# Another PSUM bank for two gate projections, one gate silu earlier on ScalarE, and the next activations loaded ahead of the weight stores

## Chip, cores and metric

The kernel runs on one core of a Trainium2 chip. The metric is the device time of one execution in microseconds; three executions of the kernel before took 3425.89 to 3429.51 us, with a median of 3427.64 us.

## What is computed

A layer over 128 sequences of 32 positions and 512 channels (4096 tokens): a conditional mixing of the 32 positions, a Mamba2-like attention part whose result is added to x, and a grouped convolution with a quantised 512x512 matrix behind it. The change lies in the attention part only:

```python
proj = jnp.einsum('bld,pd->blp', hidden_states, in_proj_w)      # gate | x, B, C | dt
xBC  = jax.nn.silu(causal_conv4(hbc))                           # 4 taps along the 32 positions
y    = scan(dt, A, x, B, C) + x * D                             # per head, 32 steps
yn   = y * rsqrt(mean(y*y over a group of 512) + eps) * norm_weight * jax.nn.silu(gate)
out  = jnp.einsum('bli,di->bld', yn, out_proj_w)
```

There are 8 groups of 512 inner channels (8 heads each); normalisation is over a group, so that the groups are independent until the output projection sums them.

## The kernel before

**Tiling.** The attention part runs 64 iterations: 8 groups (g), and in each 8 blocks of 512 tokens (j). In an iteration every engine has a program written out by hand (`attend` in `tensor_part`, `scalar_part` and `vector_part`, `scan_pass` in `gpsimd_part`, `step` in `sync_part`), and they meet through semaphores that count up over the whole kernel. Nothing is moved by a scheduler: each engine executes in the order written. `PE` is TensorE, `ACT` ScalarE, `DVE` VectorE, `POOL` GpSimd, `SP` the queue of SyncE that issues the DMAs.

**Precision.** A matrix is held as a high and a low part, and a product is three passes of matmuls (PASSES): one projection (`project(n)`, L1150 to L1157) is 12 matmuls of 512 columns into one PSUM bank, with the operands `ht` (the block's activations, turned, 2 MB, loaded by `load_h`, L984) and `wt`.

**The iteration on PE** (L1188 to L1252): projections 0 to 5 (B, C and four x tiles) into banks 0, 1, 2 in turn, with the sum of decay segments after the fourth; projections 6 and 7, the first two gates, into banks 0 and 1; the products of B and C into bank 3 (L1208); the x tiles turned into banks 4, 5, 6, 7 (`turn_x`, XT); projection 8, the third gate, into bank 2; the scan (L1172), 128 small products that write all of banks 0 to 3; the next group's raw weights turned into banks 5 and 6 (L1230, `prepare`, NEXT; not in the last group); projection 9, the fourth gate, into bank 4; and the output projection (L1249, "OUT"), for each of four channel tiles c twelve matmuls, three for each token tile t into bank OUT[t], which is (7, 5, 6, 4). Ahead of the last c the squares are turned into bank 3 (L1240). PROJ_BANK (L87) names each projection's bank.

**Waits on PE in this place.** The third gate needs bank 2 to have been read by the convolution (s_conv). The scan needs the scan matrix m (s_m), the turned x in SBUF (s_dtx), and the first three gates out of banks 0 to 2 (s_z, L1222). OUT needs for each c the low part of gy (s_ulo), and in c = 0 for bank 4 the fourth gate's silu (s_z, L1245), for banks 5 and 6 that DVE has read the turned weights (s_nlo, L1247). The next iteration's first projection needs `ht` (s_ht, L1188).

**The others.** ACT evicts a projection with its first tap (`tap`), takes silus (`silu`; `gate(c)`, L1276, from the gate's bank into z), copies the turned x to SBUF (L1320, dtx), multiplies by D (`skip`), copies the high parts (`high`, L1283; `next_high`, L1300) and squares y (`square`). DVE has the other taps, the scan matrix (L1421), y (`add_skip`, L1455), z times y (`gated`, L1463), the low parts (`low`, L1445; `next_low`, L1439), sums of squares (L1470) and, in the gaps, the decoding of an 8-bit weight table. SP issues all of the part's DMAs in order; a wait in it holds back whatever is issued later. `turn` is the last block of a group, in which the next group's weights are loaded, one by one as the projections are done.

Of the kernel before, what the change touches and what calls it, by code (L numbers as in the profile page):

```python
# [31 lines left out]
NBLK = TOK // BLK  # L32
TT = BLK // P
# [8 lines left out]
CT = GI // P  # L42
# [22 lines left out]
NCV = 2 + CT  # L65
# [18 lines left out]
CTX_AT = X2_AT + 4 * TT * DM  # L84
BIAS_AT = CTX_AT + 4 * TOK

PROJ_BANK = (0, 1, 2, 0, 1, 2, 0, 1, 2, 4)  # L87


class Shared:  # L90
# [765 lines left out]
def attend_part(nc, a, sh, ctx):  # L856
# [38 lines left out]
    sh.acc_at = TOP + WT_BYTES + HT_BYTES  # L895

    bank = sh.bank
    XT, SEG, CB, OUT, SSQ, NEXT = (4, 5, 6, 7), (4, 5), 3, (7, 5, 6, 4), 3, (5, 6)
    scanned = sh.low_banks


# [16 lines left out]
    s_proj = sem("s2_proj")  # L918
    s_tap = sem("s2_tap")
    s_cvstep = sem("s2_cvstep")  # L920
    s_conv = sem("s2_conv")
    s_silu = sem("s2_silu")
    s_z = sem("s2_z")
# [5 lines left out]
    s_dtx = sem("s2_dtx")  # L929
# [23 lines left out]
    NPJ = NCV + CT  # L953
# [26 lines left out]
    def sync_part(sp):  # L980
        acc_v = sh.acc_d.rearrange("(j t p) d -> j p t d", t=TT, p=P)

        def load_h(j):
            sp.dma_start(ht[:, :, :, :].rearrange("p a k n -> p (a k n)").bitcast(F32), sh.h_d[j]).then_inc(s_ht, 16)  # L984

        def next_chunks(j):

            return 2 + j, (j % 2 if j < NBLK - KC else NPJ + j - (NBLK - KC))

        def load_raw(g, j):  # L990
            for u, n in enumerate(next_chunks(j)):
                sp.dma_start(stage[u][:, :], weight_rows(a, n, g)).then_inc(s_raw[u], 16)

        x_v = a["x"].rearrange("b i d -> (b i) d").rearrange("(j t p) d -> j p t d", t=TT, p=P)

        def step(g, j, last, first=False):
            it = NBLK * g + j
            over = last and j == NBLK - 1
            nxt = g + 1
            turn = j == NBLK - 1 and not last  # L1000
            sp.wait_ge(s_accst, 16 * it + 16)
            if not last:
                load_raw(nxt, j)
            if turn:
                sp.wait_ge(s_nst, 32 * it + 32)
            if not first:
                sp.dma_start(acc[:, :, :], acc_v[j]).then_inc(s_accin, 16)
            if turn:
                for n in range(NPJ - 1):
                    sp.wait_ge(s_proj, NPJ * it + n + 1)  # L1010
                    sp.dma_start(wt[:, n, :, :, :].rearrange("p a k n -> p (a k n)").bitcast(F32),
                                 sh.wt_d[ds(g, 1), n].rearrange("o p n -> p (o n)")).then_inc(s_wt[n], 16)
                    if n == NCV:
                        sp.wait_ge(s_conv, NCV * (it + 1))
                        load_conv_params(nxt, sp)
            if over:
                sp.wait_ge(s_proj, NPJ * it + 7)
                sp.dma_start(sh.w4_nat[:, :, :].rearrange("p t i -> p (t i)"), sh.w4_d).then_inc(sh.s_w, 16)
                x2p_v = sh.acc_d.rearrange("(j b i) (s m) -> j s i b m", b=BLK // L, i=L, s=R)
                for h in range(2):  # L1020
                    bs = slice(h * BLK // L // 2, (h + 1) * BLK // L // 2)
                    for s in range(R):
                        sp.dma_start(sh.x2p0[s * L:(s + 1) * L, bs, 1:1 + P], x2p_v[0, s, :, bs, :]).then_inc(sh.s_x2p[0][h], 16)
                sp.dma_start(sh.x2_0[:, :, :, :].rearrange("p t r m -> p t (r m)"), acc_v[0]).then_inc(sh.s_x2[0], 16)
            if not last:
                sp.wait_ge(s_nlo, 2 * it + 2)
                for u, n in enumerate(next_chunks(j)):
                    sp.dma_start(sh.wt_d[ds(g, 1), n].rearrange("o p n -> p (o n)"),
                                 wnext[:, u, :, :].rearrange("p a n -> p (a n)").bitcast(F32)).then_inc(s_nst, 16)
            sp.wait_ge(s_proj, NPJ * (it + 1))  # L1030
            if not over:
                load_h((j + 1) % NBLK)
            if first:
                for t in range(TT):
                    sp.wait_ge(s_ulo, CT * it + t + 1)
                    sp.dma_start(z[:, t, :], x_v[j, :, t, :]).then_inc(s_xin[t], 16)
            if over:
                sp.dma_start(sh.ctx_all[:, :], sh.ctxb_d.rearrange("b o -> (b o)").partition_broadcast(P)).then_inc(sh.s_par, 16)
                sp.dma_start(sh.bias[:, :], a["L0_ffn_bias"].partition_broadcast(P)).then_inc(sh.s_par, 16)
            if turn:  # L1040
                n = NPJ - 1
                sp.wait_ge(s_nst, 32 * it + 64)
                sp.dma_start(wt[:, n, :, :, :].rearrange("p a k n -> p (a k n)").bitcast(F32),
                             sh.wt_d[ds(g, 1), n].rearrange("o p n -> p (o n)")).then_inc(s_wt[n], 16)
                sp.wait_ge(s_u, CT * (it + 1))
                load_d_norm(nxt, sp)
                sp.wait_ge(s_out, TT * (it + 1))
                for k in range(KC):
                    sp.dma_start(wot[:, :, :, k * P:(k + 1) * P].rearrange("p a c n -> p (a c) n").bitcast(F32),
                                 sh.wt_d[ds(g, 1), NPJ + k].rearrange("o p (a n) -> p (o a) n", n=P)).then_inc(s_wot, 16)  # L1050
            sp.wait_ge(s_acc, TT * it + 2 * TT)
            sp.dma_start(acc_v[j], acc[:, :, :]).then_inc(s_accst, 16)

        sp.sem_inc(s_nst, 32)
        sp.wait_ge(sh.s_turned, NWC)
        for j in range(NBLK):
            step(0, j, False, first=True)
        with sp.Fori(1, G - 1) as g:
            for j in range(NBLK):
                step(g, j, False)  # L1060
        for j in range(NBLK):
            step(G - 1, j, True)
        sp.wait_ge(s_nst, 32 * NBLK * (G - 1) + 32)
# [82 lines left out]
    def tensor_part(pe):  # L1146
        def attend(g, j, prepare):
            it = NBLK * g + j

            def project(n):  # L1150
                pe.wait_ge(s_wt[n], 16 * g + 16)
                pb = bank[PROJ_BANK[n]]
                for q, (l, rr) in enumerate(PASSES):
# [60 lines left out]
            for t in range(TT):  # L1214
                turn_x(t)

            pe.wait_ge(s_conv, NCV * it + NCV)
            project(NCV + CT - 2)

            pe.wait_ge(s_m, SEGB * it + 2 * SEGB)  # L1220
            pe.wait_ge(s_dtx, TT * it + TT)
            pe.wait_ge(s_z, CT * it + CT + 3)  # L1222
            for c in range(CT):
                ins = scan(c)
            ins.then_inc(s_yp, 1)
# [9 lines left out]
            for c in range(CT):  # L1235
                if c == CT - 1:
                    pe.wait_ge(s_y, CT * it + 2 * CT)
                    pe.wait_ge(s_sqsum, (CT - 1) * (it + 1))
                    for t in range(TT):
                        ins = pe.transpose(bank[SSQ][:, t * P:(t + 1) * P], y[:, 0, t * P:(t + 1) * P], sh.ident[:, :])  # L1240
                    ins.then_inc(s_sqturn, 1)
                pe.wait_ge(s_ulo, CT * it + c + 1)
                for t in range(TT):
                    if c == 0 and OUT[t] == PROJ_BANK[NCV + CT - 1]:
                        pe.wait_ge(s_z, CT * it + 2 * CT)  # L1245
                    elif c == 0 and prepare and OUT[t] in NEXT:
                        pe.wait_ge(s_nlo, 2 * it + NEXT.index(OUT[t]) + 1)  # L1247
                    for q, (l, rr) in enumerate(PASSES):
                        ins = pe.matmul(bank[OUT[t]][:, :], gy[:, c, l, t * P:(t + 1) * P], wot[:, rr, c, :],  # L1249
                                        start=(c == 0 and q == 0), stop=(c == CT - 1 and q == 2))  # L1250
                    if c == CT - 1:
                        ins.then_inc(s_out, 1)  # L1252
# [13 lines left out]
    def scalar_part(act):  # L1266
        def attend(g, j, prepare, first=False):
            it = NBLK * g + j
# [5 lines left out]
            def gate(c):  # L1274
                act.wait_ge(s_proj, NPJ * it + NCV + c + 1)
                act.activation(z[:, c, :], bank[PROJ_BANK[NCV + c]][:, :], ACT.Silu).then_inc(s_z, 1)  # L1276

# [3 lines left out]
            def high(c):  # L1281
                act.wait_ge(s_u, CT * it + c + 1)
                act.activation(gy[:, c, 0, :], z[:, c, :], ACT.Copy).then_inc(s_uhi, 1)  # L1283

            def square(c):
                act.activation(y[:, c, :], y[:, c, :], ACT.Square).then_inc(s_sq, 1)


            def tap(n):
                act.wait_ge(s_proj, NPJ * it + n + 1)  # L1290
                if n == 0:
                    act.wait_ge(s_cvp, 16 * NCP * g + 16 * NCP)
                act.activation(xc[:, n, :], bank[PROJ_BANK[n]][:, :], ACT.Identity, bias=cvb[:, n:n + 1],  # L1293
                               scale=cvw[:, n, TAPS - 1:TAPS]).then_inc(s_tap, 1)
# [33 lines left out]
            high(0)  # L1328
            next_high(1)
            square(0)  # L1330
            high(1)
            square(1)
            gate(3)
            high(2)
            square(2)
            high(3)
# [626 lines left out]
```

## Time and profile before

| | |
|---|---|
| runs | 3425.89, 3427.64, 3429.51 us |
| profiled execution: time, span | 3422.22 us, 3420.4 us |
| mean granted clock of TensorE | 0.997 |
| PE busy | 3325.6 us (97%) |
| DVE busy | 2610.5 us (76%) |
| ACT busy | 1762.6 us (52%) |
| POOL busy | 737.1 us (22%) |
| DMA engines, mean rate | 136 GB/s |

The span is from the first to the last instruction, and 1.8 us lie around it. A matmul's busy time contains its latency and overlaps the next one's start, so a group of matmuls "ends" in the timeline a little after the next group begins; PEld is the weight load, which runs ahead of its matmul. A line "idle before <- releaser" names what an engine waited for. The attention part is from 110 us to 3143 us, in 64 iterations.

### The profile page before, as it was taken

The page shows a single profiled execution, that of the slowest core. Times are in us where ns is not written, and L with a number is a line of the kernel's source. Part 1 is how long each engine was busy: PE and PEld are TensorE (multiplying, and loading weights), DVE is VectorE, ACT ScalarE, POOL GpSimd, SP SyncE. Part 2 cuts the span into 40 slices and gives each one's busy share as a digit, 9 for nine tenths or more (in the row PEclk, how much of TensorE's full clock was granted, in tenths as well). Part 3 has the DMA queues.
Part 4 walks back from the last instruction along what each step waited for, and adds up shares of the span by engine and source line. Part 5 has one row for each costly group of instructions (what it writes and reads, how often), then busy time and mean ns, then how long its engine had stood idle before and what let it go on. Part 6 is the DMA issues. An engine that isn't in the chain of part 4 may idle for free. (4 is left out here: it accounts for less than half of the span.)

```text
span 3420.4 us, 86449 instructions
## 1 busy us (share of the span) xinstructions
PE 3325.6 (97%) x33306; PEld 2726.9 (80%) x33306; DVE 2610.5 (76%) x4367; ACT 1762.6 (52%) x3203; POOL 737.1 (22%) x520
## 2 busy tenths in 40 slices
PE   8999999999999999999999999999999999999999
PEld 6777777778778878777788788787787877888888
DVE  6787778878787887878888777888878878787443
ACT  5666665555555555555555555555555555554111
POOL 1122221122211222112221122211122212221333
PEclk9999999999999999999999999999999999999999
DMA  7432363325533263334433253334433352224331
GB/s 268 167 116 92 135 215 130 122 104 182 174 117 123 99 220 135 123 116 159 160 135 130 109 200 119 135 133 169 145 111 135 137 171 98 74 98 154 93 92 59
DMA packets 207793, 466.29 MB, mean 136 GB/s; under 512 B 35134, under 2 KB 80606, under 8 KB 198284
## 3 DMA queue, kind: packets, MB, share of 16 engines
q1 hardware_dynamic: 206364, 464.72, 38.9%
q0 software_dynamic: 368, 0.85, 0.1%
q10 hardware_dynamic: 1024, 0.27, 0.0%
q8 instruction: 18, 0.29, 0.0%
q14 instruction: 19, 0.16, 0.0%
HBM read 313.68 MB, written 152.09 MB: 136 GB/s over the span
## 5 line engine op out<-in xcount | busy, mean ns | idle before, releaser
L1155 PE MATMUL low_banks<-ht,wt 128*128 128x512 f32 x6912 | 1616.5, 391 | 18.9 <-DMA ht<-h_d 13.6
L1155 PEld LDWEIGHTS low_banks<-ht,wt 128*128 128x128 f32 x6912 | 1289.0, 188 | 305.1 <-issue 28.2
L1403 DVE SCALAR_TENSOR_TENSOR xc<-low_banks,cvw,xc 128x496 f32<-128x496 f32 (+2 forms) x1152 | 824.1, 717 | 238.6 <-ACT xc L1293 210.5
L1249 PE MATMUL bank<-wot,gy 128*128 128x512 f32 x3072 | 749.9, 396 | 6.7
L1249 PEld LDWEIGHTS bank<-wot,gy 128*128 128x128 f32 x3072 | 562.3, 188 | 159.8 <-ACT z L1276 32.6
L1293 ACT ACTIVATE xc<-low_banks,cvb,cvw 128x512 f32<-128x512 f32 x384 | 298.5, 779 | 517.9 <-PE low_banks L1155 517.9
L1092 POOL TENSOR_TENSOR r<-rv,neg_half 128x4 f32<-128x4 f32 x64 | 98.2, 1534 | 1841.6 <-DVE rv L1493 1841.6
L1073 POOL TENSOR_TENSOR segr<-adts,mask_le 128x1024 fp32r<-128x1024 f32 x128 | 242.8, 1917 | 349.7 <-DVE adts L1394 349.7
L1272 ACT ACTIVATE xc<-xc 128x512 f32<-128x512 f32 x384 | 240.6, 626 | 140.2 <-DVE xc L1403 139.5
L1455 DVE TENSOR_TENSOR y<-xc,low_banks 128x512 f32<-128x512 f32 x256 | 174.0, 680 | 159.7 <-issue 159.7
L1283 ACT ACTIVATE gy<-z 128x512 fp32r<-128x512 f32 x256 | 161.9, 633 | 245.7 <-DVE z L1463 245.7
L1172 PEld LDWEIGHTS low_banks<-m,dtx 32*64 32x64 f32 x16384 | 169.2, 130 | 75.1 <-ACT z L1276 71.0
L1087 POOL TENSOR_TENSOR y<-y,step_of 128x512 f32<-128x512 f32 x128 | 162.8, 1291 | 299.5 <-ACT y L1309 299.5
L1172 PE MATMUL low_banks<-m,dtx 32*64 32x32 f32 x16384 | 176.5, 226 | 47.8 <-ACT z L1276 44.0
L1505 DVE SCALAR_TENSOR_TENSOR acc<-bank,r,acc 128x512 f32<-128x512 f32 x256 | 176.7, 745 | 26.2 <-ACT acc L1347 15.3
L1463 DVE SCALAR_TENSOR_TENSOR z<-z,nw,y 128x512 f32<-128x512 f32 x256 | 190.6, 745 | 6.7
L1155 PE MATMUL bank<-ht,wt 128*128 128x512 f32 x768 | 195.6, 404 | 0.0
L1445 DVE TENSOR_TENSOR gy<-z,gy 128x512 fp32r<-128x512 f32 x256 | 175.9, 687 | 13.5
L1753 PE MATMUL p_y<-wq,x3t 128*128 128x512 f32 x768 | 182.9, 394 | 0.0
L1276 ACT ACTIVATE z<-low_banks 128x512 f32<-128x512 f32 x192 | 113.5, 591 | 127.1 <-PE low_banks L1155 127.1
L1279 ACT ACTIVATE xc<-xc,dsk 128x512 f32<-128x512 f32 x256 | 171.5, 727 | 0.0
L1753 PEld LDWEIGHTS p_y<-wq,x3t 128*128 128x128 f32 x768 | 141.9, 188 | 28.3
(195 smaller groups left out, 3469.6 us busy)
## 6 DMA issues: line engine op xcount, KB each, us to landing
ht<-h_d SPq DMA_DIRECT2D x63, 2048.0 KB, 9.2
acc_d<-acc SPq DMA_DIRECT2D x64, 1024.0 KB, 4.3
wt_d<-wnext SPq DMA_DIRECT2D x112, 512.0 KB, 3.4
acc<-acc_d SPq DMA_DIRECT2D x56, 1024.0 KB, 7.0
wt<-wt_d SPq DMA_DIRECT2D x70, 512.0 KB, 7.1
stage<-in_L_attn_in_proj_w SPq DMA_DIRECT2D x84, 256.0 KB, 2.7
wot<-wt_d SPq DMA_DIRECT2D x28, 512.0 KB, 8.4
xb<-in_x SPq DMA_DIRECT2D x8, 1024.0 KB, 7.3
```

Source lines behind the costliest of these rows:

```text
L1073: pool.tensor_tensor(segr[:, half, :, :], adts[:, half, :].bitcast(F32).unsqueeze(2).to_broadcast([P, TT * HG, L]), sh.mask_le[:, :].unsqu ...
L1155: ins = pe.matmul(pb[:, :], wt[:, n, l, k, :], ht[:, rr, k, :], start=(q == 0 and k == 0), stop=(q == 2 and k == KC - 1))
L1172: ins = pe.matmul(scanned[u * HP:(u + 1) * HP, b, (c * TT + t) * L:(c * TT + t + 1) * L], dtx[rows, t, h * HP:(h + 1) * HP], m[rows, t, h, ...
L1249: ins = pe.matmul(bank[OUT[t]][:, :], gy[:, c, l, t * P:(t + 1) * P], wot[:, rr, c, :], start=(c == 0 and q == 0), stop=(c == CT - 1 and q ...
L1272: act.activation(xc[:, n, :], xc[:, n, :], ACT.Silu).then_inc(s_silu, 1)
L1293: act.activation(xc[:, n, :], bank[PROJ_BANK[n]][:, :], ACT.Identity, bias=cvb[:, n:n + 1], scale=cvw[:, n, TAPS - 1:TAPS]).then_inc(s_tap, 1)
L1403: ins = dve.scalar_tensor_tensor(dst, src, cvw[:, n, TAPS - 1 - k:TAPS - k], dst, ALU.mult, ALU.add)
L1445: dve.tensor_tensor(gy[:, c, 1, :], z[:, c, :], gy[:, c, 0, :].bitcast(F32), ALU.subtract).then_inc(s_ulo, 1)
L1455: dve.tensor_tensor(by_residue(y[:, c, :]), by_residue(xc[:, 2 + c, :]), scanned[:, :, c * P:(c + 1) * P].rearrange("p b (t l) -> p b t l" ...
L1463: dve.scalar_tensor_tensor(z[:, c, :], z[:, c, :], nw[:, c:c + 1], y[:, c, :], ALU.mult, ALU.mult).then_inc(s_u, 1)
L1505: dve.scalar_tensor_tensor(acc[:, t, :], bank[OUT[t]][:, :], r[:, t:t + 1], acc[:, t, :], ALU.mult, ALU.add).then_inc(s_acc, 1)
L1753: ins = pe.matmul(p_y[t % 2][q][:, :], x3t[:, l, t, r, :], wq[:, q, rr, r, :], start=(n == 0 and r == 0), stop=(n == 2 and r == R - 1))
```

## The change

PROJ_BANK puts the third gate into bank 4 (where the first turned x tile lay) instead of bank 2, and the fourth gate into bank 7 instead of bank 4. PE's wait ahead of the third gate is for the first turned x tile to be in SBUF (s_dtx), and the wait for the last convolution moves down to the scan, which now waits for two gates instead of three. The output banks are used in the order 4, 5, 6, 7, and in c = 0 the first of them waits for the third gate's silu, the last for the fourth's. On ACT, `gate(3)` stands behind `square(0)` instead of behind `square(1)`. On SP, `load_h` of the next block stands ahead of the wait for, and the stores of, the next group's weights.

```diff
-PROJ_BANK = (0, 1, 2, 0, 1, 2, 0, 1, 2, 4)
+PROJ_BANK = (0, 1, 2, 0, 1, 2, 0, 1, 4, 7)
...
-    XT, SEG, CB, OUT, SSQ, NEXT = (4, 5, 6, 7), (4, 5), 3, (7, 5, 6, 4), 3, (5, 6)
+    XT, SEG, CB, OUT, SSQ, NEXT = (4, 5, 6, 7), (4, 5), 3, (4, 5, 6, 7), 3, (5, 6)
...
+            sp.wait_ge(s_proj, NPJ * (it + 1))
+            if not over:
+                load_h((j + 1) % NBLK)
             if not last:
                 sp.wait_ge(s_nlo, 2 * it + 2)
                 for u, n in enumerate(next_chunks(j)):
                     sp.dma_start(sh.wt_d[ds(g, 1), n].rearrange("o p n -> p (o n)"),
                                  wnext[:, u, :, :].rearrange("p a n -> p (a n)").bitcast(F32)).then_inc(s_nst, 16)
-            sp.wait_ge(s_proj, NPJ * (it + 1))
-            if not over:
-                load_h((j + 1) % NBLK)
...
-            pe.wait_ge(s_conv, NCV * it + NCV)
+            pe.wait_ge(s_dtx, TT * it + 1)
             project(NCV + CT - 2)
 
             pe.wait_ge(s_m, SEGB * it + 2 * SEGB)
             pe.wait_ge(s_dtx, TT * it + TT)
-            pe.wait_ge(s_z, CT * it + CT + 3)
+            pe.wait_ge(s_z, CT * it + CT + 2)
+            pe.wait_ge(s_conv, NCV * it + NCV)
...
-                    if c == 0 and OUT[t] == PROJ_BANK[NCV + CT - 1]:
-                        pe.wait_ge(s_z, CT * it + 2 * CT)
+                    if c == 0 and OUT[t] in PROJ_BANK[NCV + CT - 2:]:
+                        pe.wait_ge(s_z, CT * it + CT + 3 + PROJ_BANK[NCV + CT - 2:].index(OUT[t]))
...
             square(0)
+            gate(3)
             high(1)
             square(1)
-            gate(3)
             high(2)
```

How it moves the instructions, first on PE between the turned x tiles and the first output matmuls of an iteration of the first seven groups. The names: xc the convolved tiles, ht and wt a projection's operands, m and dtx the scan's, stage the next group's raw weights, wot and gy the output projection's; low_banks are banks 0 to 3. Before:

```order
L1162 MATMUL bank7<-ident,xc_52 128x128 x4
L1155 MATMUL low_banks<-ht_58,wt_57 128x512 [waits s2_wt8,s2_conv]
L1155 MATMUL low_banks<-ht_58,wt_57 128x512 x11
L1222 REGISTER_ALU [waits s2_dtx,s2_scan_matrix]
L1172 MATMUL low_banks<-m_86,dtx_85 64x32 [waits s2_z]
L1172 MATMUL low_banks<-m_86,dtx_85 64x32 x127
...
L1155 MATMUL bank4<-ht_58,wt_57 128x512 [waits s2_wt9]
L1155 MATMUL bank4<-ht_58,wt_57 128x512 x11
L1242 REGISTER_ALU
L1249 MATMUL bank7<-wot_69,gy_82 128x512 [waits s2_ulo]
```

After:

```order
L1162 MATMUL bank7<-ident,xc_52 128x128 x4
L1217 REGISTER_ALU
L1155 MATMUL bank4<-ht_58,wt_57 128x512 [waits s2_wt8,s2_dtx]
L1155 MATMUL bank4<-ht_58,wt_57 128x512 x11
L1222 REGISTER_ALU [waits s2_dtx,s2_scan_matrix]
L1172 MATMUL low_banks<-m_86,dtx_85 64x32 [waits s2_conv,s2_z]
L1172 MATMUL low_banks<-m_86,dtx_85 64x32 x127
...
L1155 MATMUL bank7<-ht_58,wt_57 128x512 [waits s2_wt9]
L1155 MATMUL bank7<-ht_58,wt_57 128x512 x11
L1246 REGISTER_ALU [waits s2_ulo]
L1250 MATMUL bank4<-wot_69,gy_82 128x512 [waits s2_z]
```

The order of the work is the same; the bank of both gates, what each waits for, and the bank that is filled first are other.

On ACT, behind the copies of the turned weights in the same iteration (y the squares, gy the high parts). Before:

```order
L1286 ACTIVATE y_54<-y_54 128x512
L1283 ACTIVATE gy_82<-z_53 128x512 [waits s2_u]
L1286 ACTIVATE y_54<-y_54 128x512
L1275 REGISTER_ALU
L1276 ACTIVATE z_53<-bank4 128x512 [waits s2_proj]
L1283 ACTIVATE gy_82<-z_53 128x512 [waits s2_u]
```

After:

```order
L1287 ACTIVATE y_54<-y_54 128x512
L1276 REGISTER_ALU
L1277 ACTIVATE z_53<-bank7 128x512 [waits s2_proj]
L1284 ACTIVATE gy_82<-z_53 128x512 [waits s2_u]
L1287 ACTIVATE y_54<-y_54 128x512
L1284 ACTIVATE gy_82<-z_53 128x512 [waits s2_u]
```

The fourth gate's silu has moved up by one high part and one square.

On SP, around the load of the next block's activations in the first group. Before:

```order
L1028 DMA wt_d<-wnext_70 128x1024 [waits s2_nlo]
L1028 DMA wt_d<-wnext_70 128x1024
L984 DMA ht_58<-h_d 128x4096 [waits s2_proj]
L1036 DMA z_53<-in_x 128x512 [waits s2_ulo] x4
L1052 DMA acc_d<-acc_59 128x4x512 [waits s2_acc]
```

After:

```order
L984 DMA ht_58<-h_d 128x4096 [waits s2_proj]
L1031 DMA wt_d<-wnext_70 128x1024 [waits s2_nlo]
L1031 DMA wt_d<-wnext_70 128x1024
L1036 DMA z_53<-in_x 128x512 [waits s2_ulo] x4
L1052 DMA acc_d<-acc_59 128x4x512 [waits s2_acc]
```

The 2 MB load stands ahead of the two 0.5 MB stores and their wait.

## Rows read from the trace of the kernel before

**Rows 1.** The page, busy time: engine, us, share of the span, instructions
```profile
PE 3325.6 (97%) x33306; PEld 2726.9 (80%) x33306; DVE 2610.5 (76%) x4367; ACT 1762.6 (52%) x3203; POOL 737.1 (22%) x520
```

**Rows 2.** Who waited for whom, whole kernel: us in total, times, longest us
```profile
PEld bank L1249 <- ACT z L1276: 32.6, 62, 0.5
...
PE low_banks L1172 <- ACT z L1276: 44.0, 64, 0.7
...
PEld bank L1249 <- DVE wnext L1439: 11.1, 55, 0.2
PE low_banks L1155 <- DMA ht<-h_d: 13.6, 22, 1.1
...
PE low_banks L1172 <- issue: 3.8, 2, 2.0
```

**Rows 3.** Timeline of PE, one iteration's second half: start, duration, group, idle before
```profile
1658.15 3.00 PE L1155 MATMUL low_banks<-ht,wt 128*128 128x512 f32 x12
1661.83 2.74 PE L1172 MATMUL low_banks<-m,dtx 32*64 32x32 f32 x256 [0.69 <-ACT z L1276]
...
1665.35 3.02 PE L1155 MATMUL bank<-ht,wt 128*128 128x512 f32 x12
1668.21 8.82 PE L1249 MATMUL bank<-wot,gy 128*128 128x512 f32 x36
1676.87 0.60 PE L1240 MATMUL low_banks<-ident,y 128*128 128x128 f32 x4
1677.22 2.99 PE L1249 MATMUL bank<-wot,gy 128*128 128x512 f32 x12
1680.59 11.19 PE L1155 MATMUL low_banks<-ht,wt 128*128 128x512 f32 x48 [0.37 <-DMA ht<-h_d]
```

**Rows 4.** Timeline of ACT in the same iteration
```profile
1657.12 2.07 ACT L1320 ACTIVATE dtx<-bank 128x512 f32<-128x512 f32 x4 [0.38 <-PE bank L1162]
...
1661.18 0.60 ACT L1276 ACTIVATE z<-low_banks 128x512 f32<-128x512 f32 x1 [0.78 <-PE low_banks L1155]
...
1667.26 0.62 ACT L1286 ACTIVATE y<-y 128x512 f32<-128x512 f32 x1
1668.90 0.63 ACT L1283 ACTIVATE gy<-z 128x512 fp32r<-128x512 f32 x1 [1.01 <-DVE z L1463]
...
1669.95 0.58 ACT L1276 ACTIVATE z<-bank 128x512 f32<-128x512 f32 x1
```

**Rows 5.** Timeline of DVE in the same iteration
```profile
1656.66 1.29 DVE L1421 TENSOR_TENSOR m<-low_banks,y 128x512 f32<-128x512 f32 x2 [0.70 <-PE low_banks L1208]
...
1668.78 0.68 DVE L1439 TENSOR_TENSOR wnext<-bank,wnext 128x512 fp32r<-128x512 f32 x1
...
1669.98 0.68 DVE L1445 TENSOR_TENSOR gy<-z,gy 128x512 fp32r<-128x512 f32 x1
...
1675.10 0.69 DVE L1470 TENSOR_TENSOR y<-y 128x512 f32<-128x512 f32 x1
```

**Rows 6.** Timeline of SP in the same iteration
```profile
1669.64 0.91 SPq L1028 DMA_DIRECT2D wt_d<-wnext  x2
1670.69 0.62 SPq L984 DMA_DIRECT2D ht<-h_d  x1
```

**Rows 7.** Timeline of PE in the very first iteration
```profile
150.28 8.37 PE L1249 MATMUL bank<-wot,gy 128*128 128x512 f32 x36
158.49 0.60 PE L1240 MATMUL low_banks<-ident,y 128*128 128x128 f32 x4
```

**Rows 8.** Tile ht: loads' landing times, 1660 to 2770 us, then the last group
```profile
DMA to landing us min/median/max: 8.9/9.4/10.5
...
DMA to landing us min/median/max: 7.7/7.9/8.7
```

**Rows 9.** The core: span and mean granted clock
```profile
core 0: 3420.4 us, clock 0.997
```

**Rows 10.** One stretch: us, busy (x instructions) of PE, PEld, DVE, ACT, POOL, PEclk, DMA, GB/s
```profile
2804.00:2807.00 3.00, 3.00 (x8) 2.32 (x8) 2.80 (x5) 2.10 (x4) 0.00 (x0) 0.50 0.01 3
```

## The prediction

> **What bounds the kernel now.** I read the page first: TensorE is busy for 97% of the span [rows 1]. So the kernel is bound by TensorE's stream, and a change can give at most what that stream loses in gaps. The second view is therefore the list of waits, sorted by who waits [rows 2]: PE itself waits 44.0 us in 64 pieces ahead of the scan for ScalarE's silu of the third gate, and 13.6 us in 22 pieces for the activations `ht`. The weight loads of the output projection wait another 32.6 us in 62 pieces for a silu (the fourth gate's) and 11.1 us in 55 for VectorE's reading of the turned weights. All four waits lie in the second half of an iteration. The third view is the timeline of each engine there [rows 3 to 6]; the reader is to see on it who is how late, because everything that is released by the scan moves along with it.
>
> A gap costs a little more than its row says. Where nothing waits, a group's modelled end overruns the next group's start: 1665.35 + 3.02 = 1668.37, while the next begins at 1668.21 [rows 3], so 0.16 us of overlap are lost as well each time that PE waits.
>
> **Third gate in bank 4.** Before, the scan may start only when the third gate has left bank 2, since it writes banks 0 to 3. The projection ends at 1661.15, the silu runs from 1661.18 to 1661.78, the scan starts at 1661.83 [rows 3, 4]. With the gate in bank 4 the silu runs beside the scan. What the scan waits for otherwise is long done: m at 1657.95 [rows 5], the four turned tiles at 1659.19 [rows 4]; the convolution and the first two gates are ahead of these on their engines. So the next limit is PE itself, and each iteration gains 0.69 + 0.16 = 0.85 us: 64 x 0.85 = **54.4 us**. The bounds: 44.0, the rows' own time, and 55.
>
> The new wait of the third gate is for the first of the four copies that start at 1657.12 and take 2.07 together [rows 4]; a single one of this shape ends about 0.6 later, at 1657.7. PE gets there at 1658.15 [rows 3]: a margin of 0.4 us, cost nothing. Behind this wait stand all of PE's later work; if the margin vanished, each 0.1 us would cost 6.4 us. The fourth gate goes into bank 7, whose turned tile left by 1659.19: no cost. One more register instruction on PE ahead of the third gate: none of the like ahead of other projections leaves a gap, cost nothing.
>
> **Output banks and the fourth gate's silu.** Before, the last bank of c = 0 waits for a silu that runs from 1669.95 to 1670.53, behind `high(1)` and `square(1)` [rows 4]. How much do this and the wait for the turned weights cost PE, which both show only at the weight loads? The 36 matmuls take 1676.87 - 1668.21 = 8.66 us here [rows 3]. In the very first iteration, where PE had been held up and the others were ahead, they take 158.49 - 150.28 = 8.21 us [rows 7]. So both waits cost 0.45 us. By the time of the weight loads' waits, 32.6 to 11.1 [rows 2], 0.34 of it is the silu's; I take 0.38, since the other is only 0.2 at a time and partly hidden by the matmul that runs. Now the silu follows `square(0)`, which ends at 1667.88, and PE's projection, which ends at 1668.37: it runs from about 1668.4 to 1669.0, while bank 7 is wanted at 1668.21 + 9 x 0.228 = 1670.3 (0.228 being 8.21 / 36). The wait goes. Gain: 62 x 0.38 = **23.6 us**, bounds 62 x 0.34 = 21 and 62 x 0.45 = 28. The first bank's new wait is for the third silu, done seven us earlier: nothing.
>
> What is late next? The wait for the turned weights stays: VectorE ends at 1669.46 [rows 5], both it and PE hang on the scan. Then c = 1, wanted at 1668.21 + 12 x 0.228 = 1670.95, with its weight load 0.2 earlier; its low part ends at 1670.66 [rows 5]. A margin of 0.1 to 0.3; if it is missed by 0.2 in 56 iterations, 11 us come back. The sums of squares end at 1675.79 [rows 5] and PE wants them at 1676.87 - 0.38 = 1676.49: enough. `high(1)` on ScalarE started at 1668.90 for want of VectorE; now it stands behind the silu, free at about 1668.95: nothing.
>
> **The load ahead of the stores.** SP issued the stores at 1669.64 and the load at 1670.69, though the projections had ended at 1668.37 [rows 3, 6]: the load is issued 2.2 us earlier. PE's second half is shorter by 0.4 after that point, so the load is wanted at 1677.22 + 2.83 - 0.38 = 1679.67 and has some 11.2 us. It lands in 8.9 to 10.5 us with stores ahead of it, in 7.7 to 8.7 in the last group, which has none [rows 8]. Even the slowest is in time. The 22 waits go: 13.6 + 22 x 0.16 = **17.1 us**; bounds 13.6, and 18. The stores land later, behind 2 MB; who waits for them (the next iteration's `next_high`, and at a group's end the load of the fourth gate's weights, used some 40 us later) has time. At a group's end SP could issue the output weights a little late; they are wanted at the products of B and C, 22 us into the next iteration.
>
> **Sum.** 54.4 + 23.6 + 17.1 = 95.1 us. The profiled execution took 3422.2 us and would take 3327; the median of the runs stands 5.4 us above it, so I forecast 3427.6 - 95.1 = 3332 as the median. Not in the sum: in the first group PE also waits for VectorE's convolution, which hangs on loads of x behind the same queue. These may come up to 1 us earlier, or PE's shorter half may be given back there; eight iterations, -3 to +4 us.
>
> **The rivals.**
> - *The clock comes back too* (0.06). At the scan's first execution in two places PE waits 3.8 us for "issue", beside the 0.69 for the silu [rows 2], and after it TensorE's granted clock is 0.50, the 1.2 GHz level: 8 matmuls in 3 us [rows 10]. All stretches at that level in the span are worth 3420.4 x 0.003 = 10 us [rows 9]. If the shorter idle time no longer brings them about, up to half of that, 5 us, is gained too: 3327. The Trainium skill (TensorE: Matmul & The Clock Gate, What's actually happening) says that an idle array falls to the lower clock and activity releases it. By that rule fewer waits can only help, and the time would be 3327 or so instead of 3332. The rows speak against more: 64 waits of 0.69 did not bring the mean below 0.997.
> - *One term doesn't come* (0.14). The low part of c = 1, or VectorE's weights, holds up the output projection as long as the silu did (3356), or the load still lands late because loads and stores share the engines in another way (3349), or the scan finds another wait of some tenths (3345). For it: margins of 0.1 to 0.4. Against it: each margin is larger than the spread that I see between iterations.
> - *The third gate isn't freed* (0.03). If something else lets the scan start at the old time, only 41 us are left: 3387. Nothing in the rows supports it.
> - *ScalarE stuck behind the fourth gate: slower* (0.02). ScalarE executes in order, so `gate(3)` now holds `high(1)` until PE has done the fourth projection. If that came late, the low part, the output projection and everything behind would shift. The row has `high(1)` at 1668.90 and DVE taking up the low part at 1669.98; 0.4 us are hidden, 0.2 more lie ahead of PE's c = 1. To lose the 95 us, 1.5 us per iteration, and 7 more, the silu would have to end 2.2 us later than 1669.0. From there on the kernel is slower; at 3 us of delay it would be 3427.6 - 95 + 64 x 2.4 = 3486. The projection ends at 1668.37, so I see no way to it.
>
> **How the numbers follow.** The forecast itself has 0.75. Its bounds alone give 3427.6 - 101 - 4 = 3323 to 3427.6 - 79 = 3349. The range takes in the clock at the lower end with 3 us for the spread of the medians, and the single failing terms at the upper: 3318 to 3354. Below 0.2% (7 us) a measurement of this kernel can't tell a change from none. Faster by more than that 0.96, within it 0.02, slower 0.02.
>
> **What would show it.** The wait of L1172 for the silu vanishes from PE's list, and from the third gate's start to the scan's start it is 2.84 us instead of 3.68. The 36 output matmuls take 8.2 to 8.3 us, without a wait for a silu. `ht` is issued right at the end of the fourth gate's projection, and PE's waits for it are gone. PE's busy share rises to about 99%, and an iteration is 1.2 us shorter, besides the waits for ht. Wrong would be: a wait of the third gate's projection for dtx, of L1250 for gy, or an iteration shorter by under 0.8 us.

## The result, and the profile after

| | before | changed |
|---|---|---|
| median of 4 runs each | 3426.86 us | 3331.30 us |
| lowest to highest | 3425.89 to 3429.51 | 3330.59 to 3335.74 |
| profiled execution: time, span | 3422.22, 3420.4 us | 3330.75, 3329.0 us |
| PE busy | 3325.6 us (97%) | 3293.0 us (99%) |
| mean granted clock of TensorE | 0.997 | 0.997 |

The ratio is 0.9723 with a 95% interval of 0.9706 to 0.974: 95.6 us less by the medians, 91.5 us in the profiled executions. In a second comparison, beside the last experiment, the same kernel gave 0.9739 (0.9725 to 0.9753). The time lies in the forecast range, 0.7 us from the forecast.

Who waited for whom on PE (total us, times, longest us) in the changed kernel, the counterpart of [rows 2]:

```profile
PE low_banks L1155 <- DVE xc L1404: 9.3, 9, 1.9
...
PE low_banks L1172 <- issue: 4.0, 2, 2.2
...
PE bank L1250 <- DVE gy L1446: 1.2, 7, 0.2
```

The waits for the third gate's silu (44.0 us) and for ht (13.6 us) are not there any more, and the output projection waits for no silu. The first line has grown: in the kernel before PE waited for the convolution (xc) 4.8 us in 8 pieces.

The timeline of PE in the same iteration as in [rows 3], from its start:

```profile
1588.54 11.09 PE L1155 MATMUL low_banks<-ht,wt 128*128 128x512 f32 x48
...
1611.79 1.97 PE L1162 MATMUL bank<-ident,xc 128*128 128x128 f32 x16
1613.51 3.00 PE L1155 MATMUL bank<-ht,wt 128*128 128x512 f32 x12
1616.44 2.74 PE L1172 MATMUL low_banks<-m,dtx 32*64 32x32 f32 x256
...
1619.95 3.02 PE L1155 MATMUL bank<-ht,wt 128*128 128x512 f32 x12
1622.82 8.40 PE L1250 MATMUL bank<-wot,gy 128*128 128x512 f32 x36
1631.05 0.60 PE L1241 MATMUL low_banks<-ident,y 128*128 128x128 f32 x4
1631.41 3.00 PE L1250 MATMUL bank<-wot,gy 128*128 128x512 f32 x12
1634.24 2.48 PE L1155 MATMUL low_banks<-ht,wt 128*128 128x512 f32 x10
```

From the third gate's start to the scan's it is 2.93 us (3.68 before), the 36 output matmuls take 8.23 us (8.66 before), and the next iteration starts 2.83 us after the last group of twelve (3.37 before, in an iteration that waits for ht). The silu of the third gate runs beside the scan, that of the fourth ahead of the second high part, on ACT, as against [rows 4]:

```profile
1616.55 0.60 ACT L1277 ACTIVATE z<-bank 128x512 f32<-128x512 f32 x1 [0.78 <-PE bank L1155]
...
1621.87 0.62 ACT L1287 ACTIVATE y<-y 128x512 f32<-128x512 f32 x1
1623.02 0.60 ACT L1277 ACTIVATE z<-bank 128x512 f32<-128x512 f32 x1 [0.52 <-PE bank L1155]
1623.51 0.62 ACT L1284 ACTIVATE gy<-z 128x512 fp32r<-128x512 f32 x1
```

And SP issues the load 0.2 us after the output projection's start, where it was 2.5 us [rows 3, 6]:

```profile
1623.01 0.33 SPq L984 DMA_DIRECT2D ht<-h_d  x1
1624.26 0.91 SPq L1031 DMA_DIRECT2D wt_d<-wnext  x2
```

The iterations of groups 2 to 7 take 45.7 us each (47.3 before). The first group's eight take 382.1 us together (386.6 before), more than eight times 45.7, and this is where time was lost. The end of its seventh and the start of its eighth iteration on PE:

```profile
441.57 8.37 PE L1155 MATMUL low_banks<-ht,wt 128*128 128x512 f32 x36
451.89 4.61 PE L1155 MATMUL low_banks<-ht,wt 128*128 128x512 f32 x12 [1.95 <-DVE xc L1404]
```

PE waits 1.95 us for the convolution, and then twelve matmuls take 4.61 us instead of 3.00. The reason for the second stands in the granted clock of two stretches ahead of and behind the wait (columns as in [rows 10]):

```profile
445.00:449.00 4.00, 4.00 (x19) 3.31 (x18) 3.15 (x8) 3.97 (x6) 0.00 (x0) 1.00 0.00 0
452.50:455.50 3.00, 3.00 (x8) 2.30 (x7) 2.88 (x5) 1.30 (x3) 2.18 (x2) 0.50 0.59 178
```

It was at 2.4 GHz ahead of the wait and at 1.2 GHz after it.

### The profile page after: what moved, and what is told of

Same layout as the page of the kernel before. It is cut to its first block and busy times, and to the rows that moved or that the text cites. A ratio compares the mean times of both kernels' runs of the same rounds, so it can differ in the third digit from the quotient of the medians.

```text
span 3329.0 us, 86577 instructions
## 1 busy us (share of the span) xinstructions
PE 3293.0 (99%) x33306; PEld 2735.0 (82%) x33306; DVE 2609.7 (78%) x4367; ACT 1765.0 (53%) x3203; POOL 738.1 (22%) x520
## 5 line engine op out<-in xcount | busy, mean ns | idle before, releaser
L1155 PE MATMUL low_banks<-ht,wt 128*128 128x512 f32 x6144 | 1423.4, 390 | 9.3 <-DVE xc L1404 9.3
L1155 PEld LDWEIGHTS low_banks<-ht,wt 128*128 128x128 f32 x6144 | 1153.6, 188 | 258.6 <-DVE xc L1404 13.1
L1250 PE MATMUL bank<-wot,gy 128*128 128x512 f32 x3072 | 729.7, 393 | 1.2 <-DVE gy L1446 1.2
L1155 PE MATMUL bank<-ht,wt 128*128 128x512 f32 x1536 | 387.3, 401 | 0.0
L1155 PEld LDWEIGHTS bank<-ht,wt 128*128 128x128 f32 x1536 | 280.2, 189 | 55.8
L1446 DVE TENSOR_TENSOR gy<-z,gy 128x512 fp32r<-128x512 f32 x256 | 176.0, 687 | 15.2 <-ACT gy L1284 1.8
```

What stands on the lines that cost most here:

```text
L1155: ins = pe.matmul(pb[:, :], wt[:, n, l, k, :], ht[:, rr, k, :], start=(q == 0 and k == 0), stop=(q == 2 and k == KC - 1))
L1446: dve.tensor_tensor(gy[:, c, 1, :], z[:, c, :], gy[:, c, 0, :].bitcast(F32), ALU.subtract).then_inc(s_ulo, 1)
```

## The experiments

Ten runs follow, one of them of the change itself once more. All ratios are to the kernel before, which ran beside them with medians of 3421.66 to 3422.22 us (3426.86 beside the change's first run). Their intervals are 0.0013 to 0.0017 to each side (5 to 6 us), 0.001 for the silu alone, and 0.0024 (8 us) for the gate alone, whose four executions lie between 3362.73 and 3378.68 us. "Difference" is to the median of before. Where sums over an iteration's stretches are given below, they are start-to-start times of PE's timeline in the profiled executions, added up over all 64 iterations.

| third gate in bank 4 | earlier silu | load first | kernel | ratio | difference |
|---|---|---|---|---|---|
| yes | yes | yes | the change | 0.9723 and 0.9739 | -95.6 and -89.3 us |
| yes | yes | no | stores first | 0.9844 | -53.1 us |
| yes | no | yes | silu late | 0.9800 | -69.4 us |
| no | yes | yes | gate in bank 2 | 0.9882 | -40.1 us |
| yes | no | no | gate alone | 0.9850 | -50.2 us |
| no | yes | no | silu alone | 0.9986 | -4.2 us |
| no | no | yes | load alone | 0.9935 | -21.3 us |

### The stores first again

```diff
-            sp.wait_ge(s_proj, NPJ * (it + 1))
-            if not over:
-                load_h((j + 1) % NBLK)
             if not last:
                 sp.wait_ge(s_nlo, 2 * it + 2)
                 ...
+            sp.wait_ge(s_proj, NPJ * (it + 1))
+            if not over:
+                load_h((j + 1) % NBLK)
```

> The changed kernel with the weights' stores ahead of the load of ht again, as before. Theory (the load was late because it was issued 2.2 us later, behind 1 MB of stores): PE waits for ht at the start of an iteration again, and more than before, since the other two parts leave PE's second half 0.43 us shorter behind the load's issue: 29 of 48 iterations lost 0.6 us before, now some 32 us in all over groups 1 to 6; the first group gains back a few us. Time 3352 to 3362 us. Rival (with the shorter iteration the load is hidden anyway, DMA having more idle time at the end): no wait of PE for ht, 3331 us.

Measured: 3368.54 us, ratio 0.9844 (0.9828 to 0.9861). PE's list of waits:

```profile
PE low_banks L1155 <- DMA ht<-h_d: 30.4, 39, 1.8
PE low_banks L1155 <- DVE xc L1404: 5.3, 8, 0.8
```

The waits for ht are more than twice those of the kernel before. With the 0.16 us of lost overlap each, they are 30.4 + 39 x 0.16 = 36.6 us; with an early load they are nothing. The rival is out. The loss was still underestimated: 36 to 42 us by the ratios, where 21 to 31 had been expected. The traces show where it lies: the stretches from the last twelve output matmuls to the next iteration's start are 39.1 us longer than in the change, the first 48 projection matmuls of groups 2 to 8 another 3.7, and the first group's give back only 4.8.

### The silu late again

```diff
             square(0)
-            gate(3)
             high(1)
             square(1)
+            gate(3)
```

> The changed kernel with the fourth gate's silu behind high(1) and square(1) again. Theory (the silu's place on ScalarE is what held up the output bank): the 36 output matmuls take 8.6 us instead of 8.23, PEld waits 0.5 us for the silu in 62 iterations, and the time is 3331 + 62 x 0.38 = 3355 us. Rival (the bank order did it, the fourth bank now being the last in both): 3331 us.

Measured: 3352.25 us, ratio 0.98 (0.9784 to 0.9816). The weight loads' list, and PE's timeline of one iteration:

```profile
PEld bank L1250 <- ACT z L1277: 32.4, 63, 0.5
```

```profile
1680.11 8.83 PE L1250 MATMUL bank<-wot,gy 128*128 128x512 f32 x36
1688.77 0.60 PE L1241 MATMUL low_banks<-ident,y 128*128 128x128 f32 x4
```

The wait is back with 32.4 us, and 36 matmuls take 8.66 us. So it is the silu's place that held up the bank, and the order of banks is not enough: the fourth bank comes last in either order.

### The third gate in bank 2 again

```diff
-PROJ_BANK = (0, 1, 2, 0, 1, 2, 0, 1, 4, 7)
+PROJ_BANK = (0, 1, 2, 0, 1, 2, 0, 1, 2, 7)
...
-            pe.wait_ge(s_dtx, TT * it + 1)
+            pe.wait_ge(s_conv, NCV * it + NCV)
...
-            pe.wait_ge(s_z, CT * it + CT + 2)
-            pe.wait_ge(s_conv, NCV * it + NCV)
+            pe.wait_ge(s_z, CT * it + CT + 3)
```

> The changed kernel with the third gate in bank 2 again, and its old waits; the fourth stays in bank 7, the other two parts stay. Theory (the scan's wait for the third silu is a term by itself): PE waits 0.69 us in 64 iterations at L1172, third gate to scan 3.69 us instead of 2.93, and the time is 3331 + 64 x 0.76 = 3380 us. Rival (the parts overlap, so that part of it is hidden by slack behind the scan): under 3365 us.

Measured: 3381.59 us, ratio 0.9882 (0.9865 to 0.9898), so 49 to 54 us behind the change. The wait is back to the tenth:

```profile
PE low_banks L1172 <- ACT z L1276: 44.0, 64, 0.7
PE low_banks L1155 <- DVE xc L1403: 11.5, 9, 1.9
```

From the third gate's start to the scan's it is 3.68 us again, 48.5 us more over the 64 iterations. The term comes whole; nothing behind the scan had hidden a part of it.

### The gates' banks exchanged

```diff
-PROJ_BANK = (0, 1, 2, 0, 1, 2, 0, 1, 4, 7)
+PROJ_BANK = (0, 1, 2, 0, 1, 2, 0, 1, 7, 4)
...
-OUT = (4, 5, 6, 7)
+OUT = (7, 5, 6, 4)
...
-            pe.wait_ge(s_dtx, TT * it + 1)
+            pe.wait_ge(s_dtx, TT * it + TT)
```

> The changed kernel with the two gates' banks exchanged: the third gate in bank 7, the last turned tile's, so that it waits for all four copies to SBUF, the fourth in bank 4, output banks 7, 5, 6, 4. Theory (the first tile's bank is free 0.4 us ahead of need, the last one's 1.05 us behind it): PE waits 0.9 to 1.1 us ahead of the third gate in each iteration, time 3331 + 64 x 1.1 = 3401 us, so that the bank alone decides between a gain of 2.8% and one of under 1%. Rival (PE's queue waits there anyway, any of the four banks would do): 3331 us. The granted clock holds at 1.00 in spite of the wait in both.

Measured: 3404.29 us, ratio 0.9953 (0.9936 to 0.997). PE's timeline, and its list:

```profile
1740.45 1.97 PE L1162 MATMUL bank<-ident,xc 128*128 128x128 f32 x16
1743.26 3.04 PE L1155 MATMUL bank<-ht,wt 128*128 128x512 f32 x12 [0.84 <-ACT dtx L1321]
1746.23 2.74 PE L1172 MATMUL low_banks<-m,dtx 32*64 32x32 f32 x256
```

```profile
PE bank L1155 <- ACT dtx L1321: 54.0, 64, 0.8
```

From the turned tiles' start to the gate's it takes 2.81 us instead of 1.72: 1.09 us more in each of 64 iterations, 70 us. The choice among the four banks is worth 73 to 79 us: in the last tile's bank the gate waits longer than the scan did before. The mean granted clock stayed at 0.997 with this wait of 0.84 us in every iteration. The same run has a longer wait in its first group, and behind it the clock did not fall:

```profile
169.69 3.01 PE L1155 MATMUL low_banks<-ht,wt 128*128 128x512 f32 x12 [1.98 <-DVE xc L1404]
```

```profile
170.00:173.00 3.00, 3.00 (x15) 2.44 (x13) 2.89 (x5) 1.86 (x4) 2.86 (x3) 1.00 0.51 164
```

### Each part alone

The edits are those of the change, taken singly into the kernel before; for the first two the fourth gate is in bank 7 and the output banks are 4 to 7.

> The kernel before with only the third gate in bank 4 (fourth in bank 7, output banks 4 to 7; silu late, stores first). Theory: what PE gains ahead of the scan moves the issue of the load along with it, since the fourth projection and VectorE's reading of the turned weights both follow the scan; so the waits for ht stay at 14 us and the term comes whole, 49 us faster than before, ratio 0.9857. Rival (any time that PE gains is partly taken by the load): 25 to 35 us faster.

Measured: 3371.48 us, ratio 0.985 (0.9827 to 0.9874). PE waits for ht 11.8 us in 20 pieces, about as before. What PE gains ahead of the scan moves the load's issue along, and the rival (25 to 35 us) lies outside the interval of 42 to 59 us.

> The kernel before with only the output banks' order and the earlier silu (fourth gate in bank 7). Theory, after the run with the stores first lost 41 us instead of 17 (everything that shortens PE's work between the issue of the load and its use is taken back by the wait for ht where the load is late): the 36 output matmuls take 8.23 instead of 8.66 us, 26 us in all, but PE's waits for ht grow from 14 to about 30 us and more, so that only 3 to 8 us are left: ratio to before 0.998 to 0.999. Rival (terms add up): 25 us faster, ratio 0.993.

Measured: 3417.51 us, ratio 0.9986 (0.9976 to 0.9996). PE's list:

```profile
PE low_banks L1172 <- ACT z L1276: 44.0, 64, 0.7
PE low_banks L1155 <- DMA ht<-h_d: 28.8, 34, 1.8
```

The waits for ht have grown from 13.6 us in 22 pieces [rows 2] to 28.8 in 34, with the lost overlap by 15.2 + 12 x 0.16 = 17.1 us. That is not the whole: start to start, the stretches with this wait are 18.7 us longer, and the first 48 projection matmuls 3.0 us, half of it in the first group. Of the 25.4 us that the output matmuls gain, 4.2 reach the end (0.9986, 1 to 8 us by the interval).

> The kernel before with only the load of ht ahead of the stores. Theory: PE's 14 us of waits for ht go (18 us in start-to-start times), the first group gives back 3 to 6 us because its loads of x now land later behind the stores: 12 to 16 us faster, ratio 0.9955 to 0.9965. Rival (the load is worth the 41 us that its removal from the changed kernel cost): ratio 0.988.

Measured: 3400.36 us, ratio 0.9935 (0.9919 to 0.9952), 21.3 us instead of the 12 to 16 expected. No wait for ht is left, and the first group gives back only a little (PE waits 7.1 us for DVE's xc, 4.8 before). The traces tell where the rest is. The stretches with the wait are 18.6 us shorter, as expected (18). But where ht was late, the first 48 projection matmuls behind it were slower too: they took 11.00 to 11.02 us start to start (the 11.19 of [rows 3], the next group starting at 1691.61), where they take 10.93 with ht in time (the 11.09 of the changed kernel's timeline). In groups 2 to 8 that is 2.8 us more, the output matmuls add 1.3, and the first group gives back 2.3 instead of 3 to 6.

### The loads of x ahead of the stores

In the first group there is no residual in HBM yet, and SP loads x instead (four loads of 0.25 MB into z); they stood behind ht and the stores. ScalarE sorts them into acc, VectorE adds to it, and only then convolves the next projection. The edit moves them between the two:

```diff
             if not over:
                 load_h((j + 1) % NBLK)
+            if first:
+                for t in range(TT):
+                    sp.wait_ge(s_ulo, CT * it + t + 1)
+                    sp.dma_start(z[:, t, :], x_v[j, :, t, :]).then_inc(s_xin[t], 16)
             if not last:
                 sp.wait_ge(s_nlo, 2 * it + 2)
                 ...
-            if first:
-                for t in range(TT):
-                    sp.wait_ge(s_ulo, CT * it + t + 1)
-                    sp.dma_start(z[:, t, :], x_v[j, :, t, :]).then_inc(s_xin[t], 16)
```

> The changed kernel, in which the first group also issues its four loads of x ahead of the weights' stores. Theory (the first group's projections wait for VectorE's convolution, which hangs on ScalarE's sorting of x, which waits 1.5 to 3 us for loads that lie behind 1 MB of stores): ScalarE's wait for x goes from 17.7 to under 4 us, the first four projections of the first group take 11.0 to 11.5 us instead of 12.1 to 14.8, and the time falls by 8 to 12 us below the changed kernel's (ratio to before 0.969 to 0.970). Rival (the sorting's own 4.2 us are what is late): under 3 us.

Measured: 3319.42 us, ratio 0.9698 (0.9681 to 0.9714). How x landed in the changed kernel, in the tile's view from 150 to 500 us:

```profile
  DMA z<-in_x: 17.7, 8
...
DMA to landing us min/median/max: 6.9/9.5/10.8
```

and here, in the same view, where ScalarE's wait for x is gone:

```profile
DMA to landing us min/median/max: 3.9/6.5/9.0
```

In the second iteration of the changed kernel ScalarE waits 2.15 us before it sorts:

```profile
254.42 4.17 ACT L1348 ACTIVATE acc<-z 128x512 f32<-128x512 f32 x4 [2.15 <-DMA z<-in_x]
```

Here it begins to sort without a gap, and PE starts the next iteration and runs through:

```profile
251.38 4.17 ACT L1348 ACTIVATE acc<-z 128x512 f32<-128x512 f32 x4
```

```profile
249.98 2.99 PE L1250 MATMUL bank<-wot,gy 128*128 128x512 f32 x12
252.81 9.50 PE L1155 MATMUL low_banks<-ht,wt 128*128 128x512 f32 x41
```

Of PE's waits for DVE's xc one of 0.8 us is left. The first 48 projection matmuls of the first group's iterations take 88.6 us in all (100.5 in the change, 103.1 in its second run, 94.8 in the kernel before), 11.1 each, as expected. It is the loads that were late, not the sorting. This is the fastest of the kernels whose difference to the change is explained.

### The scan's waits moved into the projection

```diff
-            def project(n):
+            def scan_waits():
+                pe.wait_ge(s_m, SEGB * it + 2 * SEGB)
+                pe.wait_ge(s_dtx, TT * it + TT)
+                pe.wait_ge(s_z, CT * it + CT + 2)
+                pe.wait_ge(s_conv, NCV * it + NCV)
+
+            def project(n, before_last=None):
...
                 for q, (l, rr) in enumerate(PASSES):
+                    if q == 2 and before_last:
+                        before_last()
...
-            project(NCV + CT - 2)
-
-            pe.wait_ge(s_m, SEGB * it + 2 * SEGB)
-            pe.wait_ge(s_dtx, TT * it + TT)
-            pe.wait_ge(s_z, CT * it + CT + 2)
-            pe.wait_ge(s_conv, NCV * it + NCV)
+            project(NCV + CT - 2, scan_waits)
```

It is made on top of the kernel with x ahead of the stores. The change itself ran beside it.

> The changed kernel itself, on the chip of the other runs of this call, so that they can be compared with it: ratio to before 0.972 to 0.973. PE's start of the third gate to the start of the scan is 2.93 us, of which 0.1 stand as an issue wait of the first small weight load (0.35 us).

> The changed kernel with x loaded ahead of the stores in the first group, and with the scan's waits standing inside the third gate's projection, ahead of its last four matmuls, where all of them are met (the last copy to SBUF ends 1.0 us into the projection, these matmuls start at 1.8). Theory A (the 0.1 us ahead of the scan is the register arithmetic and the waits in PE's queue): third gate to scan takes 2.84 us instead of 2.93, the issue wait of the first small weight load goes, and the time is 6 us below the kernel with x ahead of the stores, ratio to before 0.968. Theory B (it is the change from the full array to tiles of 32 rows, whose first weights aren't loaded while a full-array matmul runs; the same 0.35 us stands ahead of the products of B and C in every iteration): 2.93 us stay, ratio 0.9698.

Measured: the change 3332.93 us, ratio 0.9739 (0.9725 to 0.9753); this kernel 3317.79 us, ratio 0.9695 (0.9682 to 0.9709). That is the same ratio as with x ahead of the stores alone, within the interval. PE's timeline and the weight loads':

```profile
1603.45 3.00 PE L1163 MATMUL bank<-ht,wt 128*128 128x512 f32 x12
1606.38 2.74 PE L1180 MATMUL low_banks<-m,dtx 32*64 32x32 f32 x256
```

```profile
1601.34 0.35 PEld L1216 LDWEIGHTS low_banks<-xc 128*32 128x32 f32 x32 [0.35 <-issue]
...
1606.38 2.63 PEld L1180 LDWEIGHTS low_banks<-m,dtx 32*64 32x64 f32 x256 [0.35 <-issue]
```

2.93 us stay, and so does the 0.35 us ahead of the first small weight load: theory A is out. Theory B is not shown. "Tiles of 32 rows" fits only one of its two places: the rows give 32x64 for the scan's weights, but 128x32 for those of the products of B and C, which have 128 rows and 32 columns. What both have in common is the step from 128x128 weights to smaller ones, and nothing here varied their size.

The Trainium skill (TensorE: Matmul & The Clock Gate, The mechanism) says that PE pulls a weight load ahead of running matmuls when it addresses other rows of the array or goes to the background weight buffer. The trace agrees for the full-array stream, which uses the same rows throughout: in the changed kernel the next iteration's weight loads start 0.22 us ahead of their first matmul (1634.24), while the twelve output matmuls still run (1631.41 + 3.00):

```profile
1634.02 2.50 PEld L1155 LDWEIGHTS low_banks<-ht,wt 128*128 128x128 f32 x11
```

Why the first small load is not pulled ahead in this way stays open.

## Why the prediction was right, and where it was not

The sum was 95.1 us; measured are 91.5 in the profiled executions, 95.6 and 89.3 by the medians. The mechanism was right: all three waits went, and each part taken back or taken alone moved the time as its wait says. That the median came within 0.7 us of the forecast is luck, since the parts erred on both sides. Start to start on PE, the traces of before and after give:

| stretch of an iteration | forecast, with its bounds | gained by the traces |
|---|---|---|
| third gate to scan | 54.4 (44 to 55) | 48.5 us |
| 36 output matmuls | 23.6 (21 to 28) | 26.1 us |
| last twelve output matmuls to the next iteration | 17.1 (13.6 to 18) | 18.6 us |
| first 48 projection matmuls, groups 2 to 8 | not in the sum | 2.5 us |
| the same, first group | not in the sum (3 gained to 4 lost) | 5.7 us lost |

- **The third gate in bank 4.** The part alone gave 50.2 us by the medians. The wait of 0.69 went whole. What was mis-sized is "the next limit is PE itself, and each iteration gains 0.69 + 0.16": of the lost overlap 0.06 came back instead of 0.16, since 0.1 is lost ahead of the scan's first small weight load, in every arrangement in which the scan didn't wait for the silu. The new wait cost nothing, as forecast, and its margin was there: the first copy ran from 1612.48 to 1613.08 and the gate started at 1613.51, 0.43 us later. In bank 7 the same gate costs 70 us.
- **Output banks and silu.** The change without the earlier silu was 20 to 26 us behind. The remaining wait for the turned weights costs less than was split off for it: 8.23 us are left against 8.21 in [rows 7], 0.02 instead of 0.07.
- **The load ahead of the stores.** All the waits went; alone it was 21.3 us. "Even the slowest is in time" held: the load has 11.2 us, and landed in 7.8 to 9.9. But 18.6 + 2.5 = 21.1 us lie outside the forecast's own bounds (13.6 to 18): PE's rows for ht leave out the shorter delays, and the projection behind a late ht was slower as well.
- **Left out of the sum: the first group.** This step failed. Its loads of x were expected up to 1 us earlier, and at worst 4 us were to be given back. They landed later, 9.5 us after their issue instead of 8.6 in the median and 10.8 instead of 9.9 at most, while PE's second half was shorter. PE's wait for the convolution went from 4.8 to 9.3 us, and 1.6 us were lost at the lower clock behind one wait of 1.95 us: 5.7 us in all, and 8.3 in the second run of the change. With x ahead of the stores the time is 8 to 14 us below the change's; that is more than the change had lost, since it also takes the waits for xc that the kernel before had.
- **The rivals.** None of them came: no term was missing, ScalarE was not stuck behind the fourth gate (the high part behind it starts at 1623.51, 0.69 after the output projection's start, exactly as before: 1668.90 - 1668.21). The clock's rival failed: both first executions of the scan still wait 4.0 us for "issue", and the mean clock is 0.997. The range was also narrower than its reason: "the single failing terms at the upper" end include 3356 us, and it stopped at 3354.

The parts aren't independent, which the sum did not say, though it used it. Alone they give 50.2 + 4.2 + 21.3 = 75.7 us, together 89 to 96. The missing 14 to 20 lie between silu and load: with the stores first, what PE gains behind the load's issue is turned into waiting for it. Gate and silu without the load give 53.1, about 50.2 + 4.2; gate and load give 69.4, about 50.2 + 21.3; silu and load give 40.1, far more than 4.2 + 21.3. The forecast came out because it costed the load by the waits before the silu was moved, and the silu with the early load in place.

## What to carry to other kernels

Where a transfer is just late, ask of each gain whether it lies ahead of the transfer's issue or behind it: ahead, it comes whole (50 us here); behind, the wait takes it back (4 of 25 us came) until the transfer is issued earlier. A PSUM bank is chosen by when its last reader is done against when the next writer arrives: here a margin of 0.4 us in one bank and a wait of 1.09 in another decided between a gain of 2.7% and one of 0.5%. And when a transfer is moved ahead in a queue, look for what else stands in that queue with a consumer that is near: no engine was seen to wait for the stores, but ScalarE waited for the loads of x behind them.

## What the runs showed of the hardware

- A wait ahead of a weight load costs the matmuls less than its row: the silu's 0.53 us of weight-load idle (32.6 us in 62 pieces) cost 0.43 us of PE's time, and the 0.19 us for the turned weights, which stayed, 0.02. A wait of PE costs more: 0.69 us shown, 0.75 us won back when it went.
- At each step from 128x128 weights to smaller ones (128x32 for the products of B and C, 32x64 for the scan) the weight loads idle 0.35 us for "issue", and PE loses 0.06 to 0.1 us: 48 projection matmuls take 10.93 us to the next 128x128 group and 11.01 to the products of B and C, twelve take 2.83 to 2.87 and 2.93. Ahead of the scan it does not depend on where the semaphores are waited for.
- One wait of 1.95 us behind full-array matmuls was followed by matmuls at the 1.2 GHz level (granted clock 0.50, twelve in 4.61 us instead of 3.00), and so were one of 1.98 us in the change's second run and one of 1.86 us with the third gate in bank 2. But the length of the wait does not decide it alone: 1.91 us in that second run and 1.98 us in the kernel with exchanged banks left the clock at 1.00 and the twelve matmuls at 3.01 us. 64 waits of 0.84 us left the mean at 0.997. The Trainium skill (TensorE: Matmul & The Clock Gate, What's actually happening) says that an idle array falls to the lower clock; the trace agrees where the clock fell, and no run here shows what decides between waits of one length.
- The loads and stores that SP issues go through one queue (464.7 of the 466.3 MB). Behind 2 MB of ht a weight store of 0.5 MB landed 9.4 us after its issue in the changed kernel, in the median of 112 (9.6 and 9.9 in two places of the first group), where ahead of it it took 3.4. The Trainium skill (DMA: Bandwidth & Descriptors, Queues, rings and completion order) says that each DMA engine takes a queue's descriptors in order; the trace agrees.
